# A sparse-attention and per-channel FFN kernel: bout on unused rows of an existing pass, one full-width s product, a regrouped sort, a relu scaled by two

## What is computed

```
queries = (x @ Wq + bq) per head;  keys, values from key_param (32 patterns)
A   = sparsemax(scale * queries . keys)          # over the 32 patterns, per head
x   = layernorm(x + (A . values) @ Wo + bo)
s   = x @ Win + bin_                              # 64 channels
h   = relu(s[..., None] * W1 + b1)                # 16 inner units for each channel
g   = sum_h(h * W2) + b2
out = layernorm(x + g @ Wout + bout)
```

## Time and profile before

| | us |
|---|---|
| median of 3 runs (1375.82 to 1378.31) | 1378.0 |
| the profiled execution | 1377.39 |
| its span, from the first to the last instruction | 1375.6 |
| PE busy | 1267.5 (92%) |
| PEld busy | 833.1 (61%) |
| DVE busy | 1129.1 (82%) |
| ACT busy | 1158.1 (84%) |
| POOL busy | 687.4 (50%) |

### The profile page before, as it was taken

One profiled execution on the slowest core, in us unless ns is written; L12 is line 12 of the kernel. 1 busy time (PEld: TensorE's weight loads), 2 busy tenths in 40 slices (PEclk: granted clock), 3 DMA queues, 4 the chain that ended last, 5 costly groups with the idle time before them and its releaser, 6 DMA issues. The chain is left out here.

```text
span 1375.6 us, 28046 instructions
## 1 busy us (share of the span) xinstructions
PE 1267.5 (92%) x6990; PEld 833.1 (61%) x6990; DVE 1129.1 (82%) x4600; ACT 1158.1 (84%) x2621; POOL 687.4 (50%) x1672
## 2 busy tenths in 40 slices
PE   7980989999999999999999999999999999799953
PEld 6650566666666666666666666666666666455431
DVE  2986888888888888888888888888888898866764
ACT  2670766789999999999999999999999999767773
POOL 1330333345555555556555555555555555556663
PEclk9995999999999999999999999999999999999975
DMA  5380676555655655655655665565565565568733
GB/s 182 91 216 16 168 224 214 182 174 181 215 186 191 215 193 185 213 196 187 209 199 184 208 203 186 203 211 188 193 214 190 188 215 185 200 196 290 252 98 69
DMA packets 91848, 258.31 MB, mean 188 GB/s; under 512 B 15731, under 2 KB 15731, under 8 KB 75286
## 3 DMA queue, kind: packets, MB, share of 16 engines
q1 hardware_dynamic: 91670, 256.39, 57.4%
HBM read 206.00 MB, written 50.33 MB: 186 GB/s over the span
## 5 line engine op out<-in xcount | busy, mean ns | idle before, releaser
L659 PE MATMUL bank<-G_sb,pT 128*128 128x512 f32 x1024 | 463.7, 596 | 2.4 <-ACT pT L754 2.4
L659 PEld LDWEIGHTS bank<-G_sb,pT 128*128 128x128 f32 x1024 | 185.7, 191 | 188.2 <-issue 185.5
L1070 DVE MAX8 top<-bank 128x8 f32<-128x32 f32 x2048 | 212.7, 182 | 39.9 <-issue 39.7
L466 POOL TENSOR_TENSOR shift_sq<-sum,per_row_sq 128x1 f32<-128x1 f32 x256 | 89.1, 348 | 281.1 <-DVE y_sb L946 278.3
L1108 DVE SCALAR_TENSOR_TENSOR acc<-hinge,w2c,acc 128x512 f32<-128x512 f32 x224 | 167.7, 749 | 65.6 <-ACT hinge L779 63.4
L767 ACT ACTIVATE unread<-y_sb,shift_sq 128x512 bf16<-128x512 f32 x256 | 184.0, 719 | 37.5 <-POOL minus_mean L468 37.2
L779 ACT ACTIVATE hinge<-s_sb,b1c,w1c 128x512 f32<-128x512 f32 x256 | 205.8, 807 | 0.2
L584 PE MATMUL bank<-A_hi,xT_hi 128*128 128x512 f32 x512 | 203.4, 397 | 0.0
L585 PE MATMUL bank<-A_lo,xT_hi 128*128 128x512 f32 x512 | 203.1, 397 | 0.0
L586 PE MATMUL bank<-A_hi,xT_lo 128*128 128x512 f32 x512 | 203.0, 397 | 0.0
L481 POOL TENSOR_TENSOR rstd<-ve,minus_half 128x1 f32<-128x1 f32 x256 | 153.1, 598 | 45.2 <-POOL ve L476 44.9
(11 more groups left out here) (128 smaller groups left out, 2510.0 us busy)
## 6 DMA issues: line engine op xcount, KB each, us to landing
G_sb<-G_of_heads SPq DMA_DIRECT2D x128, 1024.0 KB, 5.4
x_sb<-in_L_attn_query_dram SPq DMA_DIRECT2D x128, 256.0 KB, 4.7
y_sb<-in_L_attn_query_dram SPq DMA_DIRECT2D x256, 128.0 KB, 5.4
out_dram<-o_sb SPq DMA_DIRECT2D x256, 128.0 KB, 4.7
G_of_heads<-y_sb SPq DMA_DIRECT2D x64, 256.0 KB, 3.9
y_sb<-in_L_attn_Wk_dram SPq DMA_DIRECT2D x1, 1024.0 KB, 5.6
y_sb<-in_L_attn_Wq_dram SPq DMA_DIRECT2D x1, 1024.0 KB, 8.3
y_sb<-in_L_attn_Wv_dram SPq DMA_DIRECT2D x1, 1024.0 KB
```

The lines of the kernel that those rows point to most:

```text
L466: nc.gpsimd.tensor_tensor(shift_sq[:, par:par + 1], total[:, par:par + 1], per_row_sq[:], ALU.mult).then_inc(s_mean, 1)
L659: mm = nc.tensor.matmul(o_ps[i % 2][:], pT[:, bass.ds(pair_place(turn, i) + (i % H * C + c) * P, P)], G_sb[:, i % GR, c, :], start=(c == 0 ...
L1070: mx = nc.vector.max(top8[:, h, :], z_ps[i % 2][:, h * S:(h + 1) * S])
```

## The change

- The s product: Win is loaded twice, side by side, into a 128x128 piece for each c, so that one matmul for each c gives s twice for all 128 tokens, and one ACT instruction evicts it. s_sc counts 1 for each tile, not 4.
- bout: Wout_lo was multiplied by all 128 rows of `split`, whose lower half is the remainder. Now Wout_lo is zero in its lower half but for two rows with bout (rounded, and remainder), and it is multiplied by a new tile `second`: g's rounded values above, ones below. ACT makes it with one more copy for each group (s_high). L692 and bout_rows go. For the last group POOL sets A_lo[:, 0, :] to one (s_ones).
- The sort takes all 16 heads at once, with a loop of three turns over the ranks; its scratch is u_raw's second buffer and a new tile `ranked`. So the check waits until all steps so far are done (s_u).
- The relu (L864) is scaled by two, so that L1018 gives the full step; L1024 goes, and the step is subtracted.

```diff
-        Win_sb = sb("Win_sb", [P, C, M])
+        Win_sb = sb("Win_sb", [P, C, P])
-        bout_rows = sb("bout_rows", [P, D], F32R)
+        second = sb("second", [P, GROUP * P], F32R)
-        KEY_LOADS, Q_LOADS, WLOADS = 3, 2, 17
-        FILLS = 13 + S
+        KEY_LOADS, Q_LOADS, WLOADS = 3, 2, 18
+        FILLS = 14 + S
@@ loads, for each half
+                    (Win_sb[:, :, half], Win.rearrange("(c p) m -> p c m", p=P)),
@@ POOL
-            nc.gpsimd.memset(bout_rows[:].bitcast(F32), 0.0).then_inc(s_const, 1)
+            nc.gpsimd.memset(Wout_lo[:].bitcast(F32), 0.0).then_inc(s_const, 1)
+            nc.gpsimd.memset(second[:].bitcast(F32), 1.0).then_inc(s_const, 1)
+                if base + j == TILES + LAG_SCORE:
+                    pool.wait_ge(s_score, TILES)
+                    nc.gpsimd.memset(last_second.bitcast(F32), 1.0).then_inc(s_ones, 1)
-                    pool.wait_ge(s_step2, base + i + 1)
+                    pool.wait_ge(s_step, base + i + 1)
-                                            ALU.add).then_inc(s_u, 1)
+                                            ALU.subtract).then_inc(s_u, 1)
@@ PE
                     for c in range(C):
-                        for t in range(2):
-                            tokens = slice(t * HALF, (t + 1) * HALF)
-                            mm = nc.tensor.matmul(s_ps[t * M:(t + 1) * M, 0:HALF], Win_sb[:, c, :],
-                                                  yT[:, c, tokens], start=(c == 0), stop=(c == C - 1))
+                        mm = nc.tensor.matmul(s_ps[:, 0:P], Win_sb[:, c, :], yT[:, c, :], start=(c == 0),
+                                              stop=(c == C - 1))
@@
                         pe.wait_ge(s_lo, group_of(turn, i) + 1)
+                        pe.wait_ge(s_high, group_of(turn, i) + 1)
-                    nc.tensor.matmul(f[:], pick_c[:], bout_rows[:], start=True, stop=False)
-                    nc.tensor.matmul(f[:], parts[:, here], Wout_hi[:], start=False, stop=False)
-                    nc.tensor.matmul(f[:], parts[:, here], Wout_lo[:], start=False, stop=True).then_inc(s_f, 1)
+                    if base + i == LAST:
+                        pe.wait_ge(s_ones, 1)
+                    nc.tensor.matmul(f[:], parts[:, here], Wout_hi[:], start=True, stop=False)
+                    nc.tensor.matmul(f[:], high[:, here], Wout_lo[:], start=False, stop=True).then_inc(s_f, 1)
@@ ACT
-                    for t in range(2):
-                        for half in (slice(0, M), slice(M, P)):
-                            rows = slice(t * M, (t + 1) * M)
-                            nc.scalar.activation(s_sb[half, par, q * P + t * HALF:q * P + (t + 1) * HALF],
-                                                 s_ps[rows, 0:HALF], ACT.Identity,
-                                                 bias=bin_sb[rows, :]).then_inc(s_sc, 1)
+                    nc.scalar.activation(s_sb[:, par, q * P:(q + 1) * P], s_ps[:, 0:P], ACT.Identity,
+                                         bias=bin_sb[:]).then_inc(s_sc, 1)
@@
-                    nc.scalar.copy(split_of(lead)[0:M, :], both[0:M, :]).then_inc(s_hi, 1)
+                    if lead == LAST:
+                        act.wait_ge(s_ones, 1)
+                    nc.scalar.copy(split_of(lead)[0][0:M, :], both[0:M, :]).then_inc(s_hi, 1)
+                    nc.scalar.copy(split_of(lead)[1][0:M, :], both[0:M, :]).then_inc(s_high, 1)
@@
-                    nc.scalar.activation(above[:], u_raw[:, i % 2, :], ACT.Relu).then_inc(s_above, 1)
+                    nc.scalar.activation(above[:], u_raw[:, i % 2, :], ACT.Relu, scale=2.0).then_inc(s_above, 1)
@@ DVE, sort_tile after
+                nc.vector.tensor_copy(rest, scores)
+                dve.drain()
+                for h in range(H):
+                    nc.vector.max(top8[:, h, :], rest[:, h, :])
+                dve.drain()
+                nc.vector.tensor_copy(ranked[:, :, 0, :], top8[:])
+                with dve.Fori(1, S // TOP) as r:
+                    for h in range(H):
+                        nc.vector.match_replace(rest[:, h, :], top8[:, h, :], rest[:, h, :], LOWEST)
+                    dve.drain()
+                    for h in range(H):
+                        nc.vector.max(top8[:, h, :], rest[:, h, :])
+                    dve.drain()
+                    nc.vector.tensor_copy(ranked[:, :, bass.ds(r, 1), :].rearrange("p h a k -> p h (a k)"), top8[:])
+                dve.drain()
@@ DVE, the step
-                    nc.vector.scalar_tensor_tensor(step[:], sum_above[:], -1.0, twice_inv[:], ALU.add,
+                    nc.vector.scalar_tensor_tensor(step[:], sum_above[:], -2.0, twice_inv[:], ALU.add,
                                                    ALU.mult).then_inc(s_step, 1)
-                    if pool_steps(turn, j):
-                        nc.vector.tensor_scalar(step[:], step[:], -2.0, None, ALU.mult).then_inc(s_step2, 1)
-                        nc.vector.scalar_tensor_tensor(u_of(i), spread(step[:]), -2.0, by_head(u_raw[:, i % 2, :]),
-                                                       ALU.mult, ALU.add).then_inc(s_u, 1)
+                        nc.vector.tensor_tensor(u_of(i), by_head(u_raw[:, i % 2, :]), spread(step[:]),
+                                                ALU.subtract).then_inc(s_u, 1)
@@ DVE, setup in slot 1 and the check
-                    nc.vector.tensor_tensor(Wout_lo[:], Wout_sb, Wout_hi[:].bitcast(F32), ALU.subtract).then_inc(s_ready, 1)
+                    nc.vector.tensor_tensor(Wout_lo[0:M, :], Wout_sb[0:M, :], Wout_hi[0:M, :].bitcast(F32),
+                                            ALU.subtract).then_inc(s_ready, 1)
+                    nc.vector.tensor_copy(Wout_lo[M:M + 1, :], rounded.bitcast(F32)).then_inc(s_c, 1)
+                    nc.vector.tensor_tensor(Wout_lo[M + E:M + E + 1, :], bout_row, rounded.bitcast(F32),
                                             ALU.subtract).then_inc(s_c, 1)
                     dve.wait_ge(s_opens, g + 1)
+                    dve.wait_ge(s_u, so_far(turn, j, LAG_STEP))
```

More of the change, by code:

```diff
@@ L175, in build_kernel @@
         per_row_sq = sb("per_row_sq", [P, 1])
-        rest = cum[:].rearrange("p h k -> p (h k)").rearrange("p (a s) -> p a s", s=S)
-        ranked = top8[:].rearrange("p h k -> p (h k)").rearrange("p (a s) -> p a s", s=S)
+        rest, ranked = u_raw[:, 1, :].rearrange("p (h s) -> p h s", h=H), sb("ranked", [P, H, S // TOP, TOP])
         ones_s = sb("ones_s", [P, S])
-        tau_some = sb("tau_some", [P, HPC])
-        last_split = A_hi[:, 0, :]
+        last_split, last_second = A_hi[:, 0, :], A_lo[:, 0, :]
         Wk_sb, Wv_sb, Wq_sb, Wo_sb = (y_sb[:, n * C:(n + 1) * C, :] for n in range(4))
@@ L190, in build_kernel @@
         bout_row = o_sb[0:1, 2, :]
+        rounded = split[0:1, :]
         K_blk = acc[:].rearrange("p (c n) -> p c n", c=C)
@@ L224, in build_kernel @@
         s_hinge, s_acc = sem("s_hinge"), sem("s_acc")
+        s_high, s_ones = sem("s_high"), sem("s_ones")
         s_upper, s_both, s_hi, s_lo = sem("s_upper"), sem("s_both"), sem("s_hi"), sem("s_lo")
@@ L287, in split_of @@
         def split_of(lead):
-            return last_split if lead == LAST else split[:]
+            return (last_split, last_second) if lead == LAST else (split[:], second[:])
         def so_far(turn, j, lag):
@@ L354, in _ @@
                 (bo_row[:], bo.rearrange("(a d) -> a d", a=1)),
-                (Win_sb[:], Win.rearrange("(c p) m -> p c m", p=P)),
                 (bout_row, bout.rearrange("(a d) -> a d", a=1)),
@@ L803, in slot @@
                         act.wait_ge(s_lo, lead // GROUP)
+                        act.wait_ge(s_high, lead // GROUP)
                     nc.scalar.copy(both[0:M, :], acc[M:P, :]).then_inc(s_upper, 1)
@@ L912, in sort_tile @@
             def sort_tile(par, q):
-                with dve.Fori(0, H // HPC) as quarter:
-                    scores = u_sb[:, par, bass.ds(quarter * HPC, HPC), bass.ds(q, 1), :].rearrange(
-                        "p h g s -> p h (g s)")
-                    nc.vector.tensor_copy(rest, scores)
-                    dve.drain()
-                    for r in range(0, S, TOP):
-                        for a in range(HPC):
-                            nc.vector.max(ranked[:, a, r:r + TOP], rest[:, a, :])
-                        dve.drain()
-                        for a in range(HPC if r + TOP < S else 0):
-                            nc.vector.match_replace(rest[:, a, :], ranked[:, a, r:r + TOP], rest[:, a, :], LOWEST)
-                        dve.drain()
-                    for a in range(HPC):
-                        nc.vector.tensor_tensor_scan(rest[:, a, :], ones_s[:], ranked[:, a, :], 0.0, ALU.mult,
-                                                     ALU.add)
-                    dve.drain()
-                    nc.vector.scalar_tensor_tensor(rest, rest, -1.0, rank_inv[:].unsqueeze(1).broadcast_to(
-                        [P, HPC, S]), ALU.add, ALU.mult)
```

(31 more changed lines are left out.)

29 lines of the change are left out of this document (9 added, 20 removed).

## The result

The changed kernel takes 1354.0 us (median of 4 runs, 1352.8 to 1354.9), the kernel before 1377.1 (4 runs, 1375.8 to 1378.3): a ratio of 0.9834, 95% interval 0.9822 to 0.9846, 23 us faster. The forecast was 1356 in a range of 1340 to 1371; its change of -22.4 us was worked out from 1378.0, and -23.1 was measured. The profiled execution took 1352.8 us, its span is 1351.0, 24.6 less than before.

The account below looks back on a forecast made before the run. PE was taken to bound the middle, DVE's sort the early stretch, chains through ACT, POOL and DVE the end. -11.3 + 0.9 - 4.8 + 0.5 - 7.7 = -22.4 us from 1378.0 gave 1356, range 1340 to 1371.

Parts of the forecast that it names:

- PE's sum in the middle: Slots 34 to 127: bout saves 0.235, s costs 0.115 more, so 0.12 us saved per tile, 11.3 in all.
- 0.90 for the new s group: PE's s product: eight 128-column records priced at 0.90 us by a setup matmul of identical form, against 0.785 now.
- third rival: PE's full-width s product costs double, about 1.65 us for 0.785, giving 1435 us; chance 0.05.
- the fourth: PE comes out even with the s group at 1.02; only sort and chains gain, about 1367 us; chance 0.09.
- the fifth: More than one tile goes to the sort, each further one costing 25 to 30 us, about 1382; chance 0.03.
- ACT in the middle: ACT, 97% busy beside PE: 0.7 to 1 us per tile freed and an extra 0.62 copy, all hidden under PE.
- The sort: DVE's sort of one tile: 24.4 us instead of 29.2, 4.8 saved; three loop turns at 0.94; bounds nothing to 8.
- The ramp: Up to slot 22: 2.1 saved by one DVE operation, 2.2 lost to check waits, 0.4 to setup; +0.5, bounds -4 to +3.
- The end: Slots 128 to 151: 2.6 us from plain slots, 4.4 from six splits, 0.7 from one later; 7.7, bounds 2 and 16.
- The chain of the split: Last slots: ACT's copy starts 0.5 us earlier behind one short eviction, one matmul less: 0.74 at each of six splits, 4.4.
- The first rival: The end's chains close through POOL and DVE, not ACT's evictions; only 3 us there, 1360 in all; chance 0.17.
- the second: A shorter ACT queue also releases probabilities and hinges earlier; 16 us at the end, 1347 in all; chance 0.16.

Follow-up runs that it names:

- no_bias: Changed kernel without the matmul that adds the score bias, which also left no tile to sort: 1295.4 us, ratio 0.9410 to the kernel before.
- only_s: Kernel before with only the full-width s product and its one eviction: 1382.9 us, ratio 1.0042.
- bout_dve: Kernel before with only bout moved onto unused rows of the Wout_lo pass, the extra copy on DVE instead of ACT: 1363.6 us, ratio 0.9908.
- four_evictions: Changed kernel with s evicted by ACT in four 64x64 blocks again: 1367.4 us, ratio 0.9933 to the kernel before.
- only_bout: Kernel before with only bout moved onto unused rows of the Wout_lo pass, the extra copy on ACT: 1374.2 us, ratio 0.9981.
- inside_unrolled: Changed kernel with the check's wait inside the sorting branch and the sort's three loop turns written out: 1380.5 us, ratio 1.0027 to the kernel before.
- wait_inside: Changed kernel with the check's wait for the steps moved inside the branch that sorts: 1349.4 us, ratio 0.9812 to the kernel before.
- only_step: Kernel before with only the relu scaled by two and one DVE operation less in the step: 1374.9 us, ratio 0.9989.
- bout_s: Kernel before with both the s product and the bout edits, old sort and old step: 1359.9 us, ratio 0.9880.
- no_sort: Changed kernel with the sort's body left out, a pipe drain in its place: 1330.5 us, ratio 0.9668 to the kernel before.
- two_tiles: Changed kernel with each 128-column s product done as two of 64 columns, each over all 128 tokens: 1385.6 us, ratio 1.0070 to the kernel before.

## Why the prediction was right, and where its steps were not

**PE's sum in the middle: right.** The terms were -0.235 for bout and +0.115 for s, 0.12 a slot; measured 9.335 - 9.202 = 0.133, from -0.235 (no_bias prices such a matmul at 0.235) and +0.102 (only_s). From tile 36 on that made 12.1 us where 11.3 stood in the sum. The step that chose 0.90 for the new s group, by the form of L578 and not by L562, held: 0.89, and 0.81 ahead of an f product. The third rival (double price) and the fourth (PE comes out even) are out by the same rows, and the fifth (a second tile in the sort) because the trace has one sort, of 48 MATCH_REPLACE8.

**ACT in the middle: wrong, though it didn't show in the total.** The text said that work taken from ACT in this stage buys nothing. That was true of the kernel before taken as it was (only_s), and false for the change. Before, ACT's work was 194.8/200 x 9.335 = 9.09 us a slot. Without the bout matmul PE needs 9.335 - 0.235 = 9.10. The two are equal, and where ACT's work came that close (9.05 in bout_dve, 9.17 in four_evictions, 9.20 in only_bout) the slots were 9.18, 9.31 and 9.33: ACT's own work and 0.13 to 0.14 more, always with ACT at 197 of 200. So before stood only 0.1 above ACT's limit; its 2.3 us of ACT waits in 21 slots say the same. The whole change came down to 9.202 because the one eviction took ACT to 179.9/200 x 9.202 = 8.28. The prediction added an edit on PE and never asked how far PE may fall before the next engine holds it, although it had the row. For only_bout the same reckoning gave 1349, and it took 1374. That the total came out is luck in this step: the change happened to hold, next to the edit on PE, the edit on ACT that it needed.

**The sort: a term mis-sized.** 4.8 was forecast, by 24.4 us for the new body; it is 21.2, so the body gives 8.0. Of the 3.2 in between, 2.0 is the loop turns: 2.8 for three in the sum, 0.94 each from the earlier trace rows, and 0.83 measured. The rounds without turns were nearly right (forecast 14.3, and 13.75 in inside_unrolled), and what stands around them took 0.7 less than forecast. In the time the stretch from tile 12 to 16 gives 6.1, not 8.0: 0.3 is lost ahead of the sort (3.17 from the bias product of tile 12 to its first copy, 2.88 before), 0.5 from its end to MAX8 (5.6 for 5.1), and 1.1 from there to tile 16.

**The ramp: the sum about right, its terms not shown.** +0.5 was forecast; tiles 0 to 12 give -1.0 and tiles 16 to 24 +0.7 (53.3 us where it was 52.6). But the wait before the check, with the jumps that change with its place, cost 3.5 and not the 2.2 of the text, as wait_inside shows, and the operation that went gave 1.3 by only_step and not 2.1. Slots 26 to 33 lose 0.4 from tile 24 to 36 (0.9 forecast).

**The end: 6.5 against 7.7, but by another way than the text said.** It was split as 2.6 for PE's work and 4.4 for the chain of the split. The runs say: four_evictions gives 1.0 of it, only_bout 0.3, only_s 4.7, and bout_s, with the bout edit on top of only_s, 6.3. So the short eviction is worth about 5.5, and PE's work 0.3 to 1.6, little more than the noise of this column. The chain of the split itself hardly changed; ACT, POOL and PE of after there, the counterpart of the earlier trace rows:

```profile
1288.74 0.34 ACT L796 ACTIVATE s_sb<-bank,bin_sb 128x128 f32<-128x128 f32 x1
1288.86 0.75 DVE L1115 SCALAR_TENSOR_TENSOR acc<-hinge,w2c,acc 128x512 f32<-128x512 f32 x1 [0.94 <-ACT hinge L783]
...
1289.65 0.62 ACT L805 COPY both<-acc 64x512 f32<-64x512 f32 x1 [0.57 <-DVE acc L1115]
...
1290.67 1.26 POOL L512 TENSOR_TENSOR both<-acc,both 64x512 f32<-64x512 f32 x1
...
1291.96 0.62 ACT L842 CAST split<-both 64x512 fp32r<-64x512 f32 x1 [1.70 <-POOL both L512]
...
1292.66 1.26 POOL L514 TENSOR_TENSOR split<-both,split 64x512 fp32r<-64x512 f32 x1 [0.73 <-ACT split L842]
...
1293.97 0.50 PE L697 MATMUL bank<-Wout_hi,split 128*128 128x512 f32 x1 [1.10 <-POOL split L514]
```

The copy starts right behind the accumulation, as forecast. But POOL isn't free when it ends (1290.27) and starts 0.4 later, so that from the start of the last accumulation to PE's f product it is 5.11 us where it was 5.33 before: 0.2 saved and not 0.5, and PE waits 1.10 and not 0.7. Most of the tail's gain lies elsewhere, in slots 128 to 136, between the f products of tiles 94 and 102. PE of before, then of after:

```profile
1174.69 0.40 PE L693 MATMUL bank<-Wout_hi,split 128*128 128x512 f32 x1
...
1236.23 0.39 PE L693 MATMUL bank<-Wout_hi,split 128*128 128x512 f32 x1
```

```profile
1156.37 0.48 PE L697 MATMUL bank<-Wout_hi,split 128*128 128x512 f32 x1
...
1213.14 0.48 PE L697 MATMUL bank<-Wout_hi,split 128*128 128x512 f32 x1
```

It is 61.54 before and 56.77 after, 4.8 less; in only_s, with the short eviction alone, 57.04, and in four_evictions, without it, 60.23. From tile 102 to the end of the span only 1.5 us are saved. So the step that failed is the one that spread the saving over the splits of the whole tail, 0.74 at each; which wait of slots 128 to 136 the eviction shortens stays open. The first rival (nothing at the end, 1360) and the second (16 us, 1347) are both out, the second by more.

**The total: closer than its terms.** By the spans the sort and the ramp up to tile 36 gave 2.6 more than forecast, the middle 0.8 more, and the end 1.2 less. These errors partly cancel.

## What to carry to other kernels

Before an edit on the engine that is the limit is priced, work out every other engine's time for one slot: the gain ends where the next one's begins, here 0.13 us above its bare work. Two edits on two engines that are both near the limit can be worth little alone and much together (here +6.6 and -2.1 against -16.2 us), so they are to be measured as a pair; and if one edit adds work to the next engine, look for a third engine that can take it, as bout_dve did. Code behind a branch that is rarely taken cost more at each jump over it the longer it was; keep it short, and put its waits inside.

## What the hardware showed that was not expected

- An engine is full below 100% of its busy time: ACT held three kernels at 197.0 to 197.2 of 200 us, and in two of them its instructions had no idle time above 27 ns between them.
- The jump over the sort's code typically cost DVE 1.03, 1.34 or 3.62 us, more with longer code, at each of 31 checks.
- Three loop turns on DVE cost 0.83 us together (the first 0.39); the 0.94 between the quarters of the old sort was more than a turn, and what else was in it was not measured.
- In f32 a product of 64 weight columns and 64 moving columns, in 16 records, which gives s once, cost PE 0.102 us a slot less than one of 128 and 128 in eight records, which gives it twice (only_s); with 128 moving columns the 16 records cost 0.306 more (two_tiles).
- PE came back at a granted clock of 0.50 after standing still for about 5 us in no_sort, and stayed there until about 115 us, some 11 us after it had begun to work again at 104.39.
